# Graph layer on one core: one-hots written two groups of eight steps at a time, a shorter histogram, and three rebuilt chunks left out

## What is computed

```
h   = relu(layernorm(x))
summed = segment_sum(h[src], dst)          # per target node
counts = segment_sum(1, dst)
agg = summed / max(counts, 1)
x = x + log_softmax(agg @ W_l.T + h @ W_r.T + b)
# layer 1, with the edge attributes, follows on the new x
```

## Time and profile before

| | |
|---|---|
| median of three runs | 3246.06 us |
| the profiled execution: its time | 3246.28 us |
| its span, first to last instruction | 3244.4 us |
| busy: PE, DVE, ACT, POOL | 2773.8, 2649.5, 2265.0, 1767.9 us |
| counts copies, L1433 (592) | 481.3 us |
| one-hots L784, 1024 and 784 elements (592 each) | 405.5 and 339.1 us |
| dense products, L1174 (3626) | 566.9 us |
| count products, L1165 (4736) | 317.3 us |

### The profile page before, as it was taken

How to read it: one execution, slowest core, us unless ns; L and a number is a source line. 1 busy time by engine, 2 the same in 40 slices (tenths; PEclk the granted TensorE clock), 3 DMA queues, 4 the chain that set the end, 5 groups by cost and what they waited for, 6 DMA issues and landing times.

```text
span 3244.4 us, 95963 instructions
## 1 busy us (share of the span) xinstructions
PE 2773.8 (85%) x25759; PEld 2398.6 (74%) x25760; DVE 2649.5 (82%) x7484; ACT 2265.0 (70%) x5349; POOL 1767.9 (54%) x1761
## 2 busy tenths in 40 slices
PE   0789999999977777888888888899979998998987
PEld 0689999999965555777677776677767777886776
DVE  8899999999996667777777786778868887887876
ACT  2689999999735555666566665666767776776776
POOL 3311111110015777777777777777777777777750
PEclk9999999999988888999999999999999999999999
DMA  5199999991023334666566666666567767776877
GB/s 126 37 289 312 313 312 305 313 312 37 3 54 90 105 104 138 178 179 176 151 178 182 180 161 159 175 182 183 160 180 197 196 175 196 207 196 166 201 192 208
DMA packets 501352, 584.68 MB, mean 180 GB/s; under 512 B 73015, under 2 KB 472236, under 8 KB 501019
## 3 DMA queue, kind: packets, MB, share of 16 engines
q1 hardware_dynamic: 444748, 461.90, 52.4%
q0 software_dynamic: 56272, 118.81, 10.8%
HBM read 289.52 MB, written 290.92 MB: 179 GB/s over the span
## 4 chain that ended last, share of the span: by engine, by line
PE 33%; DVE 28%; issue 17%; DMA 10%; DVEq 5%; POOL 5%; ACT 2%; POOLq 0%; ACTq 0%
PE PS L1174 12%; DMA messages<-big,idxr 9%; DVE X L1059 6%; PE PS L1355 6%; PE PS L1165 5%; POOL messages L621 5%; PE PS L1293 3%; DVE aux L784 3%; PE PS L1305 2%; DVE big L980 2%; DVE big L966 2%; DVE big L977 2%; DVEq L1052 2%; DVE hpar L1046 2%; DVE big L969 2%
## 5 line engine op out<-in xcount | busy, mean ns | idle before, releaser
L621 POOL DMA_INDIRECT messages<-big,idxr x1660 | 1632.0, 983 | 587.6 <-issue 433.0
L1355 PE MATMUL PS<-big,hpar 128*128 128x128 f32 x4992 | 642.5, 283 | 112.6 <-DVE hpar L1046 90.9
L1355 PEld LDWEIGHTS PS<-big,hpar 128*128 128x128 f32 x4992 | 594.3, 195 | 161.2 <-DVE hpar L1046 129.6
L1505 ACT ACTIVATE big<-PS,b1c 128x512 f32<-128x512 f32 x415 | 284.8, 686 | 441.8 <-PE PS L1284 440.8
L1174 PE MATMUL PS<-h_parts,counts 128*128 128x258 f32 x3626 | 566.9, 296 | 0.0
L1433 ACT ACTIVATE counts<-PS 128x784 fp32r<-128x784 f32 x592 | 481.3, 825 | 95.4 <-PE PS L1165 86.0
L1293 PE MATMUL PS<-W2s,big 128*128 128x128 f32 x3320 | 479.5, 290 | 4.3 <-issue 3.1
L1059 DVE TENSOR_TENSOR X<-X,PS 128x128 f32 x1248 | 357.1, 286 | 144.3 <-DVE X L1059 10.2
L1174 PEld LDWEIGHTS PS<-h_parts,counts 128*128 128x128 f32 x3626 | 471.2, 191 | 0.2 <-ACT counts L1433 0.2
L1305 PE MATMUL PS<-hpar,big 128*128 x4980 | 415.2, 226 | 37.8 <-issue 25.4
L1293 PEld LDWEIGHTS PS<-W2s,big 128*128 128x128 f32 x3320 | 432.1, 203 | 13.6 <-issue 6.9
(11 more groups left out here) (229 smaller groups left out, 3512.8 us busy)
## 6 DMA issues: line engine op xcount, KB each, us to landing
messages<-zeros SPq DMA_DIRECT2D x875, 193.5 KB
big<-messages SPq DMA_DIRECT2D x312, 516.0 KB
aux<-slot_rows SPq DMA_DIRECT2D x415, 128.0 KB
big<-in_edge_attr_dram SPq DMA_DIRECT2D x402, 128.0 KB
messages<-big,idxr POOLq DMA_INDIRECT x1660
X<-in_x_dram SPq DMA_DIRECT2D x12, 448.0 KB, 6.9
out_dram<-X SPq DMA_DIRECT2D x6, 448.0 KB
edge_places<-big SPq DMA_DIRECT2D x1, 2496.0 KB, 13.5
```

The source lines that it names most:

```text
L621: pool.indirect_dma_start(strm_d, bass.IndirectOffsetOnAxis(ap=idxr[:, n % U, j:j + 1], axis=0), outr[:, n % U, j, :], None).then_inc(S_sc ...
L1355: last = nc.tensor.matmul(to[:, r * C:(r + 1) * C], finhot[:, n % 2, r * 2 + q, :], fin[:, k, r, q * ROW:q * ROW + C], start=(q == 0), sto ...
L1505: nc.scalar.activation(hid_to, hid_from, ACT.Relu, bias=b1c[:, :]).then_inc(S["relu_done"], 1)
```

## The change

DVE writes the one-hots of two octets (sixteen steps) with one operation per tile, so `oh_ready` counts pairs; it waits until both buffers of the pair are free. The block sums follow octets 2 and 3 in place of octet 1, the add octets 6 and 7 in place of octet 5. The histogram has 49 thresholds, that is 343 signs: 21 in each loop round of 32 octets, spread evenly over all octets, and the last seven in chunk 35. Three chunks of h (KEPT = 3) lie in front of the place where the parts begin, and are not rebuilt. The block counts' product comes two octets later.

```
-    NHS = 2 * (NCK - 5)
+    NHS = NB
+    NTHR = NHS // ((NCK - 5) // 2)
...
+        KEPT = parts_at // CW
...
+        def sign_piece(n, o, i):
+            u, ops = (n - 3) * OPC + o, NTHR * NPART
+            if i is None:
+                return (NHS - 1, o) if n == NCK - 2 and o < NPART else None
+            e = u * ops // (2 * OPC)
+            return (i * NTHR + e // NPART, e % NPART) if (u + 1) * ops // (2 * OPC) > e else None
...
-            pool.wait_ge(S["h0_high"], NCH)
-            for c in range(3):
-                h0_back(c)
             for c in range(6, NCK):
                 step_rows(c)
...
-            for c in range(3, NCH):
-                pool.wait_ge(S["h0_back"], c)
+            for c in range(KEPT, NCH):
+                wait(pool, S["h0_back"], c - KEPT)
                 h0_back(c)
...
-                wait(dve, S["counts_done"], oc - NOH + 1)
-                these = slice(o * Q, (o + 1) * Q)
+                wait(dve, S["counts_done"], c * OPC + (o - NOH + 2))
+                these = slice(o * Q, (o + 2) * Q)
+                slots = slice(o % NOH, o % NOH + 2)
...
-                    last = nc.vector.tensor_tensor(oh[:, o % NOH, :, :, :], numbers.unsqueeze(1).to_broadcast([P, Q // few, width, few]),
+                    last = nc.vector.tensor_tensor(oh[:, slots, :, :, :].rearrange("p s h l q -> p (s h) l q"),
+                                                   numbers.unsqueeze(1).to_broadcast([P, 2 * Q // few, width, few]),
...
-                    for o in range(OPB):
+                    for o in range(0, OPB, 2):
                         one_hots(c, n, h * OPB + o)
...
-                        if at and o == 1:
+                        if at and o == 2:
                             block_sums(c * 2 - 2 + h, c - 1, h)
-                        if at and o == 5:
+                        if at and o == 6:
                             add_block(c * 2 - 2 + h, h, at[h])
...
-                pe.wait_ge(S["oh_ready"], oc + 1)
+                if o % 2 == 0:
+                    pe.wait_ge(S["oh_ready"], c * (OPC // 2) + (o // 2 + 1))
...
-                        if known and c == NCK - 2 and h == 1 and o == 0:
+                        if known and c == NCK - 2 and h == 1 and o == 2:
                             block_counts()
...
-                        if not known and o >= OPB - NPART:
-                            block_signs((c - 3) * 2 + h, o - (OPB - NPART))
+                        if sign_piece(n, h * OPB + o, i) is not None:
+                            block_signs(*sign_piece(n, h * OPB + o, i))
```

More of the change, by code:

```diff
@@ L78, in gnn_program @@
     BPO = -(-NB // (OPB - 1))
-    NHS = 2 * (NCK - 5)
-    assert NCK % 2 == 1 and P // BS == 2 and N % D == 0 and SB * P == NS and LAST_COLS > 0 and NHS >= NB and NCK + SB <= 64
+    NHS = NB
+    NTHR = NHS // ((NCK - 5) // 2)
+    assert NCK % 2 == 1 and P // BS == 2 and N % D == 0 and SB * P == NS and LAST_COLS > 0 and NHS == NTHR * ((NCK - 5) // 2) + 1 and NCK + SB <= 64
     kl_d = nc.dram_tensor("edge_keys", (TP, 2 * P), fp32).ap()
@@ L381, in chunks @@
                 for k in range(2):
-                    step(i * 2 + (3 + k), 3 + k)
+                    step(i * 2 + (3 + k), 3 + k, i)
             for c in range(NCK - 2, NCK):
                 step(c, c)
+        def sign_piece(n, o, i):
[4 more added lines that the diff above has]
+            return (i * NTHR + e // NPART, e % NPART) if (u + 1) * ops // (2 * OPC) > e else None
         def half_landed(m, k):
@@ L777, in one_hots @@
             def one_hots(c, n, o):
-                oc = c * OPC + o
                 if o == 0:
                     dve.wait_ge(S["cols_ready"], c + 1)
-                wait(dve, S["counts_done"], oc - NOH + 1)
-                these = slice(o * Q, (o + 1) * Q)
+                wait(dve, S["counts_done"], c * OPC + (o - NOH + 2))
+                these = slice(o * Q, (o + 2) * Q)
+                slots = slice(o % NOH, o % NOH + 2)
                 for oh, w, width, few, numbers in ((ohl, 0, P, IL, iotaLq[:, :, :]), (ohk, 1, KD, IK, iotaKq[:, :, :])):
-                    last = nc.vector.tensor_tensor(oh[:, o % NOH, :, :, :], numbers.unsqueeze(1).to_broadcast([P, Q // few, width, few]),
+                    last = nc.vector.tensor_tensor(oh[:, slots, :, :, :].rearrange("p s h l q -> p (s h) l q"),
+                                                   numbers.unsqueeze(1).to_broadcast([P, 2 * Q // few, width, few]),
                                                    cols[:, n % 2, w, these].rearrange("p (h q) -> p h q", q=few).unsqueeze(2)
-                                                   .to_broadcast([P, Q // few, width, few]), ALU.is_equal)
+                                                   .to_broadcast([P, 2 * Q // few, width, few]), ALU.is_equal)
                 last.then_inc(S["oh_ready"], 1)
@@ L1159, in block_counts, with step_counts @@
                     .then_inc(S["hist_sum"], 1)
-            def step_counts(oc, o):
-                pe.wait_ge(S["oh_ready"], oc + 1)
+            def step_counts(c, o):
+                oc = c * OPC + o
+                if o % 2 == 0:
+                    pe.wait_ge(S["oh_ready"], c * (OPC // 2) + (o // 2 + 1))
                 wait(pe, S["counts_out"], oc - 1)
@@ L1184, in _, with layer0 @@
             step_columns(0, 0)
-            def layer0(c, n):
+            def layer0(c, n, i=None):
                 known = isinstance(c, int)
@@ L1194, in layer0 @@
                             pe.wait_ge(S["wT_ready"], 1)
-                        step_counts(c * OPC + (h * OPB + o), h * OPB + o)
+                        step_counts(c, h * OPB + o)
                         if o and (not known or c * 2 + h >= 1):
@@ L1218, in node_transposes @@
             def node_transposes(c):
-                pe.wait_ge(S["h0_back"], c + 1)
+                wait(pe, S["h0_back"], c + 1 - KEPT)
                 transposes(c, lambda i: H[:, c * CB + i, :], "h0T_done")
@@ L1413, in column_copy @@
                 act.wait_ge(S["kT_done"], m + 1)
-                wait(act, S["oh_ready"], (m - 1) * OPC)
+                wait(act, S["oh_ready"], (m - 1) * (OPC // 2))
                 nc.scalar.activation(cols[:, n % 2, :, :], psK.rearrange("p (w e) -> p w e", w=2), ACT.Copy).then_inc(S["cols_ready"], 1)
@@ L1481, in first_part @@
                 act.wait_ge(S["prod_done"], c + 1)
-                act.wait_ge(S["h0_back"], NCH)
+                act.wait_ge(S["h0_back"], NCH - KEPT)
                 nc.scalar.activation(hp[:, chunk(c), 0, :], psP[:, 0:CW].rearrange("p (b c) -> p b c", c=C), ACT.Copy)\
```

## The result

The changed kernel takes **3198.27 us** (median of four runs, 3195.75 to 3199.2) against 3245.59 (3244.36 to 3248.88) for the kernel before, measured beside it: a ratio of 0.9848 [0.9836, 0.9859], 47.3 us less. The forecast was 3194, the range 3186 to 3222.

The account below looks back on a forecast made before the run. Layer 0's loop was taken as bound by a PE-DVE-PE round trip stalling PE each half; loop -43.9, rebuilding -6.4, chunks 1 and 2 -2.4, chunk 0 +0.2 sum to -52.5: 3246.3 to 3194, range 3186 to 3222.

Parts of the forecast that it names:

- The round trip: Layer 0 loop: PE to DVE to PE closes once per half; without its stall 19.65 us per chunk instead of 20.94.
- late release: Rival: handovers with 0.26 to 0.28 us to spare fail, 0.3 us stall stays per half, 3214 us; chance 0.17.
- The size of merging: DVE's one-hots in pairs of steps: 1.98 us per pair instead of 2.16, bounds 1.81 to 2.16.
- The loop: Chunks 3 to 36 of layer 0: 34 x 1.29 = 43.9 us less, upper end 46.3.
- hidden: The block counts' product, moved by two steps, is the same product and was given no cost.
- The rebuilding: Near 162 us, a DVE one-hot operation takes 6.92 us while POOL rebuilds three chunks; without them 6.4 us less.
- Chunks 1 and 2: DVE's stretch before the loop: 16 pairs x 0.18, less some 0.5 waiting: 2.4 us less, 0 to 5.6 by bounds.
- Chunk 0: Ends with ACT's zeroing after step 8, which now also waits for step 9's one-hots: 0.2 us more, -0.9 to +1.1.
- The thresholds: ACT's 105 fewer signs (61 us of ACT) remove nothing from today's path; they keep ACT from being next.
- Outside the change: The tail and layer 1 are untouched: forecast difference 0 before the first transpose and after layer 0.
- The slower case: Rival: the merged operation loses two elements per cycle, a pair takes 4.0 us, about 3700 us; chance 0.04.
- the round trip stays: Rival: DVE still reaches PE last in each half, the loop gains only 6 us, 3231 us; chance 0.09.

Follow-up runs that it names:

- x2: The changed kernel with the three rebuilt chunks put back on POOL between the gathers: 3208.37 us, ratio 0.9881.
- x1: The changed kernel with the old 64 thresholds, 14 signs per chunk behind octets 1 to 7: 3200.33 us, ratio 0.9857.
- x4: The changed kernel with the block sums after octets 0 and 1 and the add after octets 4 and 5: 3336.26 us, ratio 1.0273.
- b1: The kernel before with only the block sums moved after octet 3 and the add after octet 7, one-hots per octet: 3211.35 us, ratio 0.9886.
- x3: The changed kernel with one one-hot operation per octet and tile, same order, waits and releases per pair: 3239.71 us, ratio 0.9971.

## Why the prediction was right

- **The round trip** was read right. That a half would run at 9.72 and 9.93 us without the stall came from PE's own starts, and came true to 0.01. The handovers with 0.26 and 0.28 us to spare held, so no late release: DVE has time to wait before its pairs (0.17 in the rows above, 0.48 in the next half, at 514.75).
- **The size of merging**: 2.02 us per pair for 1.98. The slope held, as 480 elements still cost 0.24 us, 0.5 ns each; the saving per pair is 0.14, not 0.18. By the 151 cycles of the Trainium skill, page "VectorE: DVE Perf Modes", section on the TRN2 errata, an estimate from its formula for fp32, it would be 0.31; the starts decide against that as a price per operation in a busy queue. DVE needs 8 x 2.02 + 2 x (0.85 + 0.33) + 0.2 = 18.7 us per chunk, the figure of the forecast.
- **The loop**: -43.33 for -43.9. Most of the 0.57 is the step that called the block counts' product *hidden* because it is "the same product". It stands alone now: `813.13 0.74 PE L1166` delays the next octet by 0.58 us, and that half takes 10.29. Before, its time fell into the stall: that half took 10.37, where the others took 10.31. A stall that goes uncovers what it hid.
- **The rebuilding**: -6.4 forecast, 6.0 and 6.6 by the two runs. The Trainium skill, page "SBUF — State Buffer", section "SBUF: two separate sides", was set aside as reading zero. x2 is kinder to it: POOL's record begins first (160.64, DVE's at 160.87), and each DVE operation is held for about one of POOL's, as an exclusive lock for a whole instruction would do. In the kernel before, DVE's operation has the earlier record (162.34, its forerunner's ending at 162.41) and POOL's begins at 162.65; whether records 0.3 us apart show who came first at the port is not shown by any run. Why one operation of DVE was held through all three of POOL's there stays open.
- **Chunks 1 and 2** were the weakest term: -6.99 for -8.8 with the rebuilding. The merging gave less there than 16 x 0.18, by the measured 0.14 it is 2.24. Some 0.9 us of the miss lie in the mark, PE's first count product of chunk 3: it now has to wait for a whole pair of one-hots, which starts it 2.44 us after DVE's first operation in that chunk (168.76 to 171.20), before 1.57 (175.72 to 177.29). And at the start of chunk 3 DVE idles longer before it adjusts the next keys: 1.21 us without a releaser (168.76), 0.43 before. The add is now the last operation in the chunk, and the instructions that load the addresses follow it with nothing to cover them; that these are the reason is argued from the order, not tested.
- **Chunk 0**: -0.95 for +0.2. ACT's zeroing began at 95.59, 0.89 later than before, but PE had begun 1.85 later. The five pairs up to that point took DVE 12.31 us (81.55 to 93.86), where nine octets had taken 13.27 (79.70 to 92.97). Both are slower than in the loop, while POOL works too, and there a pair saves not 0.18 but 0.49 us (2.46 for 2.95).
- **The thresholds** were costed at nothing, rightly, but the reason given, that the cut keeps ACT from being next, fell with x1. The step that was wrong is the price of a sign: 0.58 us was read where ACT keeps PE's pace (0.72 + 0.58 = 1.30, the distance of PE's octets), so it holds a wait. Where the next counts are there, a sign with its read-out takes 0.40 to 0.53 by its length, and 14 of them with 16 copies and a column copy some 18.3 us per chunk (an estimate from these starts), not 19.6 and that copy.
- **Outside the change**: +1.85 ahead of the first transpose, which lay between 77.8 and 79.3 over the other kernels, and +2.4 after layer 0, where those without the extra pauses lie between 2341.5 and 2353.3. Both are of the size of the scatter between programs and runs, and with them the total came out 4 us above the forecast.
- **The rival that was missed.** The slower case was looked for in the rate of the merged operation, which the slope in the earlier trace rows spoke against. The real way to lose was the order: x4 costs 138 us against the changed kernel. The rival "the round trip stays" was priced at 3231, a small gain; with pairs the stall grows by an octet's one-hots and a second one comes up before octet 6, and the kernel that keeps the old order took 3336.

## What to carry to other kernels

When two engines both show 95% busy, look for a loop of waits that closes once per block, and first move the consumer's work behind what the other engine needs next; merging instructions makes such a loop longer, and paid here only after the move. Read an instruction's price where its engine has nothing to wait for: next to an engine with a steady pace, the distance of two starts is that pace. Take a stall's length from the starts on the engine that stalls, and list what stood in its shadow, because it will be paid for. When a stretch that an edit does not touch gets longer by a fixed amount per loop round, with idle time that nothing releases and more instruction packets, shift the program by some instructions before believing any theory about data.

## What had not been expected of the hardware

The place of DVE's loops costs as much as half of this change: pauses of 4.9 to 5.9 us at each jump back of one loop, 20 more instruction packets, 26 to 36 us in all, for 112 instructions more ahead of it, and none at 256. The Trainium skill, page "Runtime: NRT & Kernel Launch", section "Instruction fetch mechanics", says that instructions come in blocks of 256 and that a jump to a place outside the two blocks at hand has to wait for a fetch. The traces agree: a shift of 256 instructions took the pauses away, and 20 packets come and go with them. No run tests another whole block, and the price is theirs.

POOL's gather of the loop changed its length with DVE's order of work, at the same work of its own: 2.05 us for each before, 3.48 after, 4.85 in b1, 3.90 in x3, and 0.95 in x4. The length of DVE's operations doesn't decide, since b1 and x3 have the short ones. The rows of the changed kernel (POOL, then DVE's add), of b1 and of x4:

```profile
509.15 3.48 POOL L545 DMA_INDIRECT KLg<-edge_keys,tj_i  x1 [16.17 <-PE PS L1153]
```

```profile
511.73 0.42 DVE L812 TENSOR_TENSOR big<-big,PS 128x256 f32 x1
```

```profile
498.53 4.86 POOL L535 DMA_INDIRECT KLg<-edge_keys,tj_i  x1 [14.97 <-PE PS L1145]
```

```profile
506.58 0.95 POOL L545 DMA_INDIRECT KLg<-edge_keys,tj_i  x1 [22.57 <-PE PS L1153]
```

In the changed kernel, as in b1 and x3, the gather ends 0.9 us after the add that breaks DVE's row of one-hots has started (511.73 to 512.63 here, 502.46 to 503.39 in b1), and in x4 DVE waits for PE through all of its 0.95 us. So it seems to stand until DVE's one-hots break off; no run was made to test this. POOL idles about 15 us or more before each, so nothing was lost here; a kernel whose gathers are due sooner would pay for a long row of one-hots on DVE.
